# A float32 tower on one core: mixer and attention as two stages or as one block

## What is computed

```python
# token mixer
y = emb[x] + pos
q, k, v = y @ Wq + bq, y @ Wk + bk, y @ Wv + bv
a = softmax(q @ k.T) @ v @ Wo + bo
y = layernorm2d(y + a, ln1_w, ln1_b)            # mean and variance over a whole sequence
f = gelu((y @ W1 + b1) @ W2 + b2)
h = layernorm2d(y + f, ln2_w, ln2_b)
# attention, 12 heads of 16
q, k, v = split(layernorm(h) @ qkv_w.T + qkv_b)
w = softmax(rms_norm(q) @ rms_norm(k).T / 4)
h = h + (w @ v) @ proj_w.T + proj_b
# mixture of experts with two levels of slots
h = h + ffn(layernorm(h), gamma_in, slots1, ...)
```

## Time and profile before

| what | value |
|---|---|
| median of 3 runs | 594.68 us (592.46 to 597.42) |
| the profiled execution | 597.51 us |
| its span | 595.5 us |
| mean granted TensorE clock | 0.977 |
| matmul busy (PE) | 549.3 us, 92% |
| VectorE busy (DVE) | 316.9 us, 53% |
| ScalarE busy (ACT) | 258.0 us, 43% |
| GpSimd busy (POOL) | 86.4 us, 14% |

### The profile page before, as it was taken

One profiled execution on the slowest core, in us unless ns is written; L12 is line 12 of the kernel. 1 busy time (PEld: TensorE's weight loads), 2 busy tenths in 40 slices (PEclk: granted clock), 3 DMA queues, 4 the chain that ended last, 5 costly groups with the idle time before them and its releaser, 6 DMA issues. The chain is left out here.

```text
span 595.5 us, 13808 instructions
## 1 busy us (share of the span) xinstructions
PE 549.3 (92%) x5571; PEld 449.4 (75%) x5571; DVE 316.9 (53%) x734; ACT 258.0 (43%) x821; POOL 86.4 (14%) x132
## 2 busy tenths in 40 slices
PE   6998896899999999999966889999989999999997
PEld 5887785876566665666854665788878999999996
DVE  3266728646677677665135744446652434443443
ACT  1233332334665667644345637546662322332230
POOL 6534000001101332130125100001000000000000
PEclk9997898999999999999988999999998999999999
DMA  6450000000000000000090006000006999999833
GB/s 226 129 184 1 2 0 1 1 2 1 1 2 2 2 1 2 1 2 2 23 409 6 1 2 198 1 2 2 1 1 235 410 331 335 338 335 338 252 55 113
DMA packets 20723, 58.81 MB, mean 99 GB/s; under 512 B 3043, under 2 KB 9797, under 8 KB 20549
## 3 DMA queue, kind: packets, MB, share of 16 engines
q1 hardware_dynamic: 14756, 49.47, 22.5%
q0 software_dynamic: 1056, 4.33, 4.0%
q10 hardware_dynamic: 4848, 4.13, 2.4%
HBM read 53.21 MB, written 4.33 MB: 97 GB/s over the span
## 5 line engine op out<-in xcount | busy, mean ns | idle before, releaser
L1999 PE MATMUL banks<-slots_t,w 64*128 64x128 f32 x1536 | 91.4, 272 | 1.1 <-PEq L1694 1.1
L1999 PEld LDWEIGHTS banks<-slots_t,w 64*128 64x128 f32 x1536 | 90.1, 188 | 1.6 <-issue 1.3
L1127 DVE TENSOR_REDUCE qk<-banks 128x4 f32<-128x1024 f32 x48 | 58.8, 1226 | 42.5 <-PE banks L791 42.5
L2072 ACT ACTIVATE ex_gelu<-banks,b_sb 128x128 f32<-128x128 f32 x128 | 36.5, 368 | 90.1 <-PE banks L1999 90.1
L791 PE MATMUL banks<-qk_t 16*128 16x256 f32 x384 | 54.4, 400 | 0.6 <-DVE qk L1127 0.4
L798 PE MATMUL banks<-qk_t 17*128 17x256 f32 x384 | 54.4, 400 | 0.0
L2092 DVE SCALAR_TENSOR_TENSOR ex_act_t<-banks,b_sb,ex_gelu 128x128 f32<-128x128 f32 x128 | 36.0, 344 | 29.2 <-ACT ex_gelu L2072 29.2
L2030 PE MATMUL banks<-w,ex_act_t 64*128 64x192 f32 x512 | 47.1, 323 | 1.0 <-DVE ex_act_t L2092 1.0
L96 PE MATMUL banks<-ident 128*128 128x128 f32 x348 | 45.9, 279 | 1.3 <-PEq L102 1.0
L791 PEld LDWEIGHTS banks<-qk_t 16*128 16x128 f32 x384 | 33.0, 184 | 18.3 <-issue 9.7
L96 PEld LDWEIGHTS banks<-ident 128*128 128x128 f32 x348 | 41.6, 192 | 5.7 <-issue 5.7
(11 more groups left out here) (227 smaller groups left out, 1045.0 us busy)
## 6 DMA issues: line engine op xcount, KB each, us to landing
w<-in_w SPq DMA_DIRECT2D x32, 768.0 KB, 10.2
w<-in_w2e SPq DMA_DIRECT2D x32, 384.0 KB, 11.3
w_slot<-in_w_slot SPq DMA_DIRECT2D x8, 576.0 KB, 3.8
rows_scratch<-ex_rows ACTq DMA_DIRECT2D x28, 96.0 KB, 7.3
yn_all<-rows_scratch POOLq DMA_DIRECT2D x7, 384.0 KB, 9.6
out<-h SPq DMA_DIRECT2D x8, 192.0 KB, 1.9
qkv_w_sb<-in_qkv_w SPq DMA_DIRECT2D x1, 864.0 KB
wk_t<-in_wk_t ACTq DMA_DIRECT2D x2, 289.5 KB, 3.6
```

The source lines that it names most:

```text
L1127: nc.vector.tensor_reduce(to, flat(MAXES[0], MAXES[1] + 1).rearrange("p (h t n) -> p h t n", h=2, n=SEQ), AX.X, ALU.max, negate=True).then ...
L1999: return nc.tensor.matmul(bank[:, j * P:(j + 1) * P], g.w1[n % BUFS][rows, first + j * P:first + (j + 1) * P], x, start=start, stop=stop, ...
L2072: nc.scalar.activation(gelu[n % 2][:, j * P:(j + 1) * P], gate_bank(n)[:, j * P:(j + 1) * P], ACT.Gelu_apprx_tanh, bias=g.t["b1"][:, n, HB ...
```

## The change

`token_mixer` and `attention` become one function and one block, `mixer_and_attention`, with no common wait between them. Attention's tiles that were its own (`prob`, `out_t`, `sq`, `x`, `x_t`, `mixed`) now lie in the mixer's weight tiles, which are no longer used by then. LAST is body 1.

*Loads and GpSimd.* The slots are loaded before the wait for the keys, attention's weights directly behind it, in front of `w1_t` and `w2`. GpSimd presets `val` and `qk` first, prepares `qkv_w` when its own loads are there, and adds the positions for body 1 only once the first norm's variance is ready. It also scales sequence 0:

```diff
             sp.wait_ge(tok["keys"], WIDE)
-            sp.dma_start(slots_raw[:, :], g.d["slots1"]).then_inc(loaded_slots, 16)
+            for name in FRONT_OPERANDS:
+                sp.dma_start(g.t[name], g.d[name]).then_inc(front_loaded, 16)
             sp.dma_start(w1_t[:, :, :], g.d["w1_t"]).then_inc(loaded_mlp, 16)
...
-            pool.wait_ge(g.operands_loaded, 16 * N_OPERANDS)
+            pool.wait_ge(front_loaded, 16 * len(FRONT_OPERANDS))
...
             for i in range(1, BATCH // WIDE):
+                pool.wait_ge(tok["var_ready"], norms(i - 1, 0))
                 place(i)
...
-            for n in range(1, BATCH):
+            for n in range(BATCH):
                 pool.wait_ge(S["rms_rooted"], n + 1)
```

*TensorE.* Three of body 1's four keys stand in front of the norm's matmul of body 0; the last norm's statistics use bank 5 instead of 7. In body 1, `turn_x(0)` stands between the scores of sequences 1 and 2, the projections of sequence 0 stand behind the mix, in front of the norm's matmul, and `turn_x(1)` behind the MLP. The fillers of the mixer's end, of attention's start and of `body(0)` are gone:

```diff
                     last.then_inc(tok["scores"], 1)
+                    if i == LAST and s == 1:
+                        turn_x(0)
...
+                if i == LAST:
+                    make_qk(0)
+                    make_qk_rest(0)
+                    make_v(0)
+                    make_v_rest(0)
                 norm_stats_pe(pe, i, 0)
...
                 if more:
                     for s in range(WIDE):
                         turn(i + 1, s)
+                    for s in range(WIDE - 1):
+                        keys(i + 1, s)
                 else:
-                    keep_busy(nc, g, 1, 8)
+                    turn_x(1)
                 norm_stats_pe(pe, i, 1)
-                if not more:
-                    keep_busy(nc, g, 1, 18)
...
                 if more:
+                    keys(i + 1, WIDE - 1)
...
-            keep_busy(nc, g, 0, 8)
-            turn_x(0)
-            keep_busy(nc, g, 0, 3)
-            make_qk(0)
-            make_qk_rest(0)
-            keep_busy(nc, g, 0, 6)
-            make_v(0)
-            make_v_rest(0)
-            keep_busy(nc, g, 0, 3)
-            turn_x(1)
             for quad in range(QUADS):
                 fill_quad(0, quad)
             scores_and_maxima(None, (0, 0, 0))
-            keep_busy(nc, g, OUT[1], 4)
```

*ScalarE.* The slots' norm moves in front of body 0. Body 1 gets these parts of the front:

```diff
+                if i == LAST:
+                    root_var(0)
                 for s in range(WIDE):
                     act.wait_ge(tok["values"], at(i, s))
...
+                    if i == LAST and s == 1:
+                        keep_x(0)
+                if i == LAST:
+                    root_var(1)
+                    keep_qk(0)
+                    keep_v(0)
...
                 nc.scalar.preload_act_table_set(EXP_LN)
                 if more:
                     for s in range(WIDE):
                         turned_copy(i + 1, s, 0, 2 * s)
+                else:
+                    root_rms(0)
+                    keep_x(1)
                 root(i, 1)
```

```diff
+            variance(LAST, 1)
             keep_fill(0)
             row_max(0, 0, 0)
             for n in range(BATCH):
                 body(n)
+                if n < WIDE:
+                    centre(LAST, 1, n)
+                    scale(LAST, 1, n)
```

More of the change, by code:

```diff
@@ L336, in keys, with token_body @@
                 last.then_inc(tok["keys"], 1)
[L338 to L341, removed]
+            def token_body(i, more):
                 for s in range(WIDE):
@@ L860, in project, with warm @@
                 last.then_inc(S["projected"], 1)
-            def warm(n, first, last):
-                if n == 0 and first:
-                    keep_busy(nc, g, OUT[1], first)
+            def warm(n, last):
                 if n == BATCH - 1 and last:
@@ L914, in body @@
                     turn_x(n + 2)
-                warm(n, 0, 4)
+                warm(n, 4)
                 turn_max(n, 2)
                 mix(n, 1)
-            pe.wait_ge(g.qkv_bias_set, 32)
-            keep_busy(nc, g, 0, 8)
-            turn_x(0)
-            keep_busy(nc, g, 0, 3)
-            make_qk(0)
-            make_qk_rest(0)
-            keep_busy(nc, g, 0, 6)
-            make_v(0)
-            make_v_rest(0)
-            keep_busy(nc, g, 0, 3)
-            turn_x(1)
+            fold_qk()
+            pe.wait_ge(g.ident_made, 1)
+            turn(0, 0)
+            fold(1, 0)
+            fold(1, 1)
+            turn(0, 1)
+            turn(0, 2)
+            keys(0, 0)
+            keys(0, 1)
+            turn(0, 3)
+            keys(0, 2)
+            keys(0, 3)
+            for i in range(BATCH // WIDE):
+                token_body(i, more=i + 1 < BATCH // WIDE)
             for quad in range(QUADS):
@@ L986, in keep_v @@
                 act.wait_ge(S["v_made"], n + 1)
+                if n == 0:
+                    for t in range(TPS):
+                        last = nc.scalar.copy(val[0][:, t, :, 0:HDIM],
+                                              g.ps[FIRST_V[t]][:, 0:DIM].rearrange("p (h d) -> p h d", d=HDIM))
+                    last.then_inc(S["v_kept"], 1)
+                    return
                 nc.scalar.copy(val[n % 2][:, :, :, 0:HDIM],
@@ new lines, in stats @@
+            def stats(i, which):
+                for s in range(WIDE):
+                    dve.wait_ge(tok["stats1"], 2 * nth(i, s, which))
+                    nc.vector.bn_aggr(stat[:, s, :], tok_bn[s][:, :, :]).then_inc(tok["stats2"], 1)
+                dve.wait_ge(tok["stats2"], WIDE * norms(i, which))
+                nc.vector.tensor_tensor(mean_sq[:, :], stat[:, :, 0], stat[:, :, 0], ALU.mult
+                                        ).then_inc(tok["squared"], 1)
+                dve.wait_ge(tok["squared"], 2 * norms(i, which) - 1)
+                nc.vector.tensor_tensor(stat[:, :, 1], stat[:, :, 1], mean_sq[:, :], ALU.add
+                                        ).then_inc(tok["stats3"], 1)
@@ new lines, in token_norm, with keep_keys @@
+            def token_norm(i, which):
+                for s in range(WIDE + 1):
+                    if s < WIDE:
+                        centre(i, which, s)
+                    if s:
+                        scale(i, which, s - 1)
+            def keep_keys(i, s):
+                dve.wait_ge(tok["keys"], at(i, s))
+                nc.vector.tensor_copy(key_t[s][:, :, :], g.ps[2 * s + 1][0:AUG, :].rearrange("p (c n) -> p c n", c=2)
+                                      ).then_inc(tok["keys_kept"], 1)
```

679 lines of the change are left out of this document (321 added, 358 removed).

## The result

The changed kernel takes 599.89 us (median of 15 runs, 594.78 to 603.48), the kernel before 595.89 (15 runs in the same comparison, 592.46 to 599.56): ratio 1.0066, 95% interval 1.0045 to 1.0087. The forecast was 586.0, in a range of 579 to 592. The change costs some 4 us where it was to win 9. The profiled execution took 599.89 us, its span is 597.9 and the mean granted clock 0.951, where before had 595.5 and 0.977.

The account below looks back on a forecast made before the run. TensorE, busy 92% of the span, was taken as the bound, winnable only where it idles, runs at half clock or works for nothing. 13.1 + 0.5 - 2.0 - 0.8 - 2.2 = 8.6 us gain: 586.0, range 579 to 592.

Parts of the forecast that it names:

- part 8: Attention's fills and start of body 0: run at half clock after TensorE's idle stretch; -2.2 us, cost between 0 and 3.4.
- Rival B: Mixer's MLPs of bodies 0 and 1 wholly cold, attention cold for two long stretches: gain only 3.0 us, 591.7; chance 0.18.
- rival C: Attention stays at half clock past body 0; through body 1 it gives 603, 601 against the median; chance 0.04.
- a digit of 5 beyond 125 us: TensorE's clock digit on the profile page, after attention's start: a 5 there would show the forecast wrong.
- Parts 1 to 4: Path from the keys of mixer body 1 to attention's first fill of quads: fill at 115.7 instead of 128.8, gain 13.1 us.
- Part 3: Second half of mixer body 1: MLP can start 0.7 us sooner, partly at half clock, end taken as before at 110.4.
- Part 5: Attention's body 0: fillers removed, only some of whose ends were in the way; +0.5 us, between 0 and 2.8.
- Part 6: Ends of attention's bodies: two VectorE norm operations added, 0.65 to 0.7 us exposed three times; -2.0 us.
- Part 7: Mixer's body 0: earlier start, but GpSimd's position additions collide with VectorE's norm, MLP starts at 56.9; -0.8 us.
- Rival A: Mixer's body 0: no collision, GpSimd is held instead of VectorE; gain 14.6 us, 580.1; chance 0.2.

Follow-up runs that it names:

- Experiment 1: Changed kernel with fillers back around the mixer's last norm matmul, ahead of attention's body 0 and in its pauses: 593.68 us, ratio 0.9956.
- experiment 4: Kernel before without its fillers at the mixer's end, around attention's front and in attention's body 0: 604.96 us, ratio 1.0118.
- experiment 7: Changed kernel with fillers added only in the five pauses and at the end of the first slots' stage: 595.14 us, ratio 0.9978.
- experiment 6: Changed kernel with the edits of experiments 1, 2 and 3, plus fillers in the first slots' stage: 580.73 us, ratio 0.9731.
- experiment 9: Changed kernel unaltered, profiled again: 599.64 us; and the kernel of experiment 7 with 40 more fillers behind the first slots' stage: 602.52 us.
- experiment 2: Changed kernel with the last norm's two VectorE operations moved from the end to the middle of attention's bodies: 596.45 us, ratio 1.0006.
- experiment 3: Changed kernel with GpSimd's position additions released behind the norm's last operation in the mixer's body 0: 594.76 us, ratio 0.9961.
- experiment 8: Changed kernel with fillers only around the mixer's last norm matmul: 600.88 us; with those of attention's body 0 only: 596.14 us.

## Why the prediction was wrong

It failed in one step, part 8, "Clock after the fill", which took 2.2 us for what measured 8.9, and in what the sum left out behind it. The sign that the prediction named for rivals B and C, a digit of 5 beyond 125 us, came. The base moved by 1.2 us as well (594.7 from three runs, 595.89 from 15).

- **Part 8, -2.2 forecast, -8.9 measured.** I sized the fall by the lengths of the stretches that the kernel before shows, 3.4 and 6.8 us. This one lies over the fill and the short products that wait for VectorE's maxima, and it lasted 27.3 us: +2.8 us from fill to first mark, +6.1 in body 0. That is rival C's mechanism, a clock that stays down in body 0, at a price of 0.33 us per us of half clock (8.9 / 27.3), not 0.45. I gave it 0.04, for "in the earlier trace rows no stretch lasted over 6.8": evidence from a kernel that had 60 fillers around just that place. Experiment 1 gives the whole 8.9 back, experiment 4 brings a fall without the change. That the fall comes from the missing fillers is shown. Why it lasts 27.3 us is not: with the same body 0, also without fillers, the clock was back after two stretches of 3.4 us in the profile of experiment 7, and soon after the first mark in experiment 4.
- **Left out: the first slots' stage.** My sum stopped at attention's body 0 and took all behind it as before. It added 4.7 us, from stretches of half clock that its 1.8 us pauses bring (before 306.8 to 310.3 and 313.7 to 317.1; after 300.3 to 310.6 and three more). Experiments 6, 7 and 9 show that the pauses bring them; why there are more of them after the change is not shown.
- **Parts 1 to 4, right.** Value mix at 88.39 for 88.8; the norm's matmul directly behind the projections at 97.19 for 98.0; the fill at 115.47 for 115.7. The mixer's body 1 began 0.6 us sooner (its first transposes at 62.59 for 63.18), so 12.75 of the 13.35 us are theirs, for 13.1. Part 3 too: the MLP started 0.76 sooner and was colder, 6.43 us for 5.90, with its end near 110.1.
- **Part 5, +0.5: wrong in kind.** I saw only that some fillers end in the way. What they hold up is the clock of the work behind them: experiment 1 is faster with them, and experiment 4 loses 7 us without.
- **Part 6, -2.0 forecast, -2.4 measured** (0.8 per body instead of 0.65 to 0.7), and wholly given back by experiment 2. My point that VectorE has spare time in certain places only was the right one.
- **Part 7, -0.8 forecast, +0.6 measured.** The MLP of body 0 started at 56.75 for 56.9, but it was less slowed by the clock than I took (5.8 us to the next transposes, for 5.2 before). The engines alternate as argued: four of VectorE's operations last 1.35 us instead of 0.61 (one of them within the pair at 48.21), and GpSimd's four 5.06 us. The norm ended some 0.8 us sooner than I had it, since GpSimd was done before VectorE was. Rival A was priced well, MLP at 52.7 in its bound and 52.72 in experiment 3, but it is not what the chip does by itself. The Trainium skill, page "SBUF — State Buffer", section "Who interferes with whom", lets issue order decide who blocks. The trace agrees only for one instruction at a time: with work waiting on both engines neither keeps the port. VectorE's four start 1.27 us apart (48.74, 50.01, 51.28, 52.56), and GpSimd's four take 1.27 each.
- **Rival B** had the right cause, the clock, but only half in the right place: of its 5.6 us, 2.8 were for attention, and 2.8 for the MLPs of body 0 and body 1, which lost only 0.6 and 0.5 us to it.

Put together: 13.35 - 8.9 - 2.4 = 2.05 us won at attention's end, 4.7 lost behind it.

## What to carry to other kernels

Before fillers are removed as useless, find out what the clock does without them: on a dependent chain they were worth 7 to 9 us here, where I had counted 0.5 against them, and half a set of them did not do so reliably. A gain in one stage can be followed by more half clock in a stage behind it that has regular pauses, here 4.7 us; so hold the clock there first and compare the two kernels after that. Vector operations added to a loop belong where the engine waits, not where it is convenient to write them: 1.2 us per body cost 0.8 at the end of a body and nothing in the middle.

## What was not expected of the hardware

TensorE stayed at half clock while it was busy for 26.43 of 27.3 us, and for 33.43 of 34.1 us (experiment 8). Its matmuls there were short ones with few rows of the array in use (16x256, 17x256) between longer ones. The same products run at full clock in attention's later bodies, so they alone don't hold the clock down; what does was not tried. The same kernel has two times 8 us apart on one chip, 586.9 and 595.1, by whether the clock comes back early. The Trainium skill, page "TensorE: Matmul & The Clock Gate", section "What's actually happening", says that the clock's watch runs on its own and doesn't start with the kernel, so that the transition varies from run to run. The runs agree that the moment of the transition varies from run to run; why it does, none of them shows. The 8.2 us are 1.4% of this kernel.
